# The third layer's setup of a four-layer cross-attention kernel, regrouped by token tile and by head

## The chip, the cores and the metric

The kernel runs on one core of a Trainium2 chip. The metric is the device time of one execution in microseconds (us). The engines are TensorE (PE in the profile, with PEld for its weight loads), VectorE (DVE), ScalarE (ACT), GpSimd (POOL) and SyncE (SP, which here only starts DMAs). They run side by side and wait for one another on semaphores.

## The reference, cut to what matters

Four gated cross-attention layers, each followed by a feed-forward part, work on x of 8 x 56 tokens by 128 features, with a context of 8 x 1500 tokens. The change lies in the attention of the third layer, between the second layer's experts and the loop over the context:

```python
x = layer_norm(ctx, ...)                     # per context token, done earlier in the kernel
latents = layer_norm(x_tokens, ...)
q = latents @ Wq                             # 448 x 512: 8 heads of 64
k, v = split(concat([x, latents]) @ Wkv)     # per head 64 wide
q = q / |q| * q_scale                        # norm of each token and head
k = k / |k| * k_scale
sim = einsum(q, k) * 8                       # masked softmax over 1500 + 56 keys
out = softmax(sim) @ v
```

The kernel never forms the keys in this loop. For head h it uses q_h (W_k,h c) = (W_k,h^T q_h) c, so each head's normalised query (64 rows) is multiplied once by that head's key weights (64 x 128), and the loop then multiplies the 128-row result with the normalised context. The norms of the keys are applied to the scores.

## The kernel before

The 448 tokens stand in 4 token tiles of 112 (`TT` = 112, `NT` = 4, `N` = 448); `H8` = 8 heads, `HD8` = 64, `D` = 128. `ps` is the matmul memory, 8 banks of 512 words per partition, indexed as `ps[partition, bank, column]`.

The setup of the third layer is one chain. DVE normalises the latents; PE turns them, DVE copies them to `xT`. PE multiplies `xT` with `w_q2` (token tile t to bank t) and then with `w_k2` (tile t to bank 4 + t). ACT squares the query tiles one by one into `big2`; DVE waits for all four query products (`product_in.next(4)`), sums the squares by head (4 reductions), ACT takes the root, DVE the reciprocal, and one DVE multiplication over all four banks (112 x 2048) writes the normalised queries to `big`. PE turns them by 16 transposes, feature chunk c (two heads) to bank c. In each chunk partitions 0 to 63 hold the even head of the pair and 64 to 127 the odd one; ACT copies partitions 64 to 127 and DVE partitions 0 to 63, each in one instruction over four banks, into `qT2` of 8 heads, whose other halves GpSimd has zeroed by a memset (`l2_zero`). Because of the zeros, the product for a head takes all 128 rows of `w_kT2[:, h // 2, :]`. The 8 products go to the 8 banks, signalled after the fourth and the eighth. ACT casts each to float16 (`qtT[:, 0]`), DVE subtracts that from the float32 product to get the float16 remainder (`qtT[:, 1]`). Ahead of its subtractions DVE also does the norms of the latents' own keys: a reduction of 112 x 2048, a maximum, ACT's root, a reciprocal.

Then comes the loop over 8 batches of 13 key tiles (`sim2`, `scale2`, the exponential, `pv2`, and GpSimd's sum of the probabilities `psum2`). Its first scores need both halves of `qtT` and the loads of the first batch (`l2_ld`), which SP starts once the latents are stored.

`op.next()` on PE waits for the next count of the semaphore `operand`, which DVE raises; `product_in.next()` and `act_in.next()` on DVE do the same for `product` (raised by PE) and `from_act` (raised by ACT). `ch.step` counts a DVE instruction, `signal(s)` waits for the counted ones and raises `s`. `keep_clock(n, k)` issues n float16 matmuls of 128 x 512 into bank k whose result nobody reads. Each engine works through its instructions in the order of the program. A float32 matmul stands in the trace as two instructions.

Of the kernel before, what the change touches and what calls it, by code (L numbers as in the profile page):

```python
# [11 lines left out]
ALU = mybir.AluOpType  # L12
# [3 lines left out]
D = 128  # L16
B = 8
S = 56
N = B * S
NT = 4  # L20
TT = N // NT
# [100 lines left out]

PRODUCT = {"latent_q": 14, "latent_k": 18, "latent_qT": 19, "queries2": 20, "queries3T": 27}

# [6 lines left out]

OPERAND = {"latentsT": 13, "x3T": 24}

# [59 lines left out]
def build(nc, io, out):  # L193
    ctx = ExitStack()
    with ctx:
# [3 lines left out]
        def sem(name):  # L199
            return ctx.enter_context(nc.semaphore(name))  # L200
# [164 lines left out]
        ctxT = carve([D, H8, N])  # L365
        qT2 = ctxT
        sscl = [carve([KP, N]) for _ in range(2)]
# [95 lines left out]
        ld_rn = sem("latent_key_norms_loaded")  # L463
        l2_zero = sem("l2_queries_zeroed")
        l2_kn = sem("l2_latent_key_norms")
# [244 lines left out]
        def _(pe):  # L710
# [365 lines left out]
            for w in (w_q2, w_k2):  # L1076
                for t in range(NT):
                    mm = pe.matmul(ps[0:TT, t if w is w_q2 else 4 + t, :], xT[:, TT * t:TT * t + TT], w,
                                   start=True, stop=True)
                    if w is w_q2 or t == NT - 1:  # L1080
                        mm.then_inc(product, 1)
            op.next()
            for c in range(4):
                for t in range(NT):
                    mm = pe.transpose(ps[0:D, c, TT * t:TT * t + TT], big[:, t, D * c:D * c + D],
                                      ident[0:TT, 0:TT])
            mm.then_inc(product, 1)
            op.next()
            for h in range(H8):
                mm = pe.matmul(ps[0:D, (4 + h) % 8, 0:N], w_kT2[:, h // 2, :], qT2[:, h, :], start=True, stop=True)  # L1090
                if h % 4 == 3:
                    mm.then_inc(product, 1)
            op.next()
# [215 lines left out]
        def _(act):  # L1309
# [179 lines left out]

            act.wait_ge(product, PRODUCT["latent_qT"])  # L1490
            act.wait_ge(l2_zero, 1)
            act.copy(qT2[64:D, 1::2, :], ps[64:D, 0:4, 0:N]).then_inc(from_act, 1)
            act.wait_ge(to_act, 3)
            act.activation(qss[:, 1, :], qss[:, 1, :], ACT.Sqrt).then_inc(from_act, 1)
            for half in range(2):
                act.wait_ge(product, PRODUCT["queries2"] + half)
                for h in range(4 * half, 4 * half + 4):
                    act.copy(qtT[:, 0, h, :], ps[0:D, (4 + h) % 8, 0:N]).then_inc(qt_hi, 1)
            with act.Fori(0, B // 2) as i:
# [80 lines left out]
        def _(pool):  # L1580
# [99 lines left out]
            rsqrt()  # L1680
            pool.memset(qT2, 0.0).then_inc(l2_zero, 1)

# [70 lines left out]
        def _(dve):  # L1753
# [4 lines left out]
            def tt(out, a, b, op):  # L1758
                return dve.tensor_tensor(out, a, b, op)  # L1759

            def over(col, shape):

                return col.unsqueeze(2).broadcast_to(shape)
# [482 lines left out]
            signal(lat_ready)  # L2246
            product_in.next(4)
            for t in range(NT):
# [6 lines left out]
            ch.link(dve.reciprocal(qss[:, 2, :], qss[:, 2, :]))  # L2255
            bigf = big.rearrange("p t (h d) -> p (t h) d", h=H8)
            tt(bigf, ps[0:TT, 0:4, :].rearrange("p t (h d) -> p (t h) d", h=H8),
               over(qss[:, 2, :], [TT, NT * H8, HD8]), ALU.mult).then_inc(operand, 1)
            product_in.next(2)
            dve.wait_ge(l2_zero, 1)  # L2260
            ch.step(dve.tensor_copy(qT2[0:64, 0::2, :], ps[0:64, 0:4, 0:N]))
            act_in.next(5)
# [5 lines left out]
            for h in range(H8):  # L2268
                if h % 4 == 0:
                    product_in.next()  # L2270
                dve.wait_ge(qt_hi, h + 1)
                ch.step(tt(qtT[:, 1, h, :], ps[0:D, (4 + h) % 8, 0:N], qtT[:, 0, h, :], ALU.subtract))
            signal(operand)

# [232 lines left out]
```

## Time and profile before

| | |
|---|---|
| device time, median of 3 runs | 846.31 us (844.57 to 850.4) |
| profiled execution: device time | 849.31 us |
| profiled execution: span from first to last instruction | 847.5 us, 15714 instructions |
| PE, PEld busy | 754.1 us (89%), 496.9 us (59%) |
| DVE, ACT, POOL busy | 608.8 us (72%), 411.9 us (49%), 338.3 us (40%) |
| mean granted TensorE clock | 0.940 of full speed |
| the third layer's setup, from the latents' first product to the loop's first scores | 383.13 to 407.45 us of the span |

Busy shares are averages over stages with different limits, so the change is read from its own stage: which instruction released the next, and when. Times in the rows are us from the start of the span. The granted clock is 1.00 at 2.4 GHz and 0.50 at 1.2 GHz.

### The profile page before, as it was taken

What the parts mean: (1) busy time and instruction counts of PE and PEld (TensorE: products, weight loads), DVE (VectorE), ACT (ScalarE), POOL (GpSimd) and SP (SyncE); (2) the same over time, 40 slices, a digit from 0 to 9 for tenths busy, and PEclk for the clock granted to TensorE, in tenths of its full rate; (3) what the DMA queues carried; (4) which work ended last, traced back from release to release, by engine and by line L of the source; (5) the groups of instructions that cost most, each with busy time, mean ns of one, the idle gap of its engine ahead of it and who ended that gap; (6) DMA issues with size and microseconds to landing.
All of it is one profiled execution on the core that took longest, in us unless ns stands there. A gap on an engine that the chain in (4) does not pass through costs nothing.

```text
span 847.5 us, 15714 instructions
## 1 busy us (share of the span) xinstructions
PE 754.1 (89%) x5632; PEld 496.9 (59%) x5632; DVE 608.8 (72%) x1264; ACT 411.9 (49%) x675; POOL 338.3 (40%) x271
## 2 busy tenths in 40 slices
PE   4699999996778988997899999997799998998997
PEld 3577777785445475653455555563346665655575
DVE  4889999997887755565655556658789997525653
ACT  2476666673465524424445444421127775834331
POOL 0665555553523601540587787732241211100111
PEclk9899999997998968999999999998959999998999
DMA  7256766532425530206022233006746677000320
GB/s 202 94 193 216 244 211 202 162 122 84 55 85 183 159 108 0 84 29 173 1 77 76 78 110 106 8 14 100 111 84 132 123 147 157 3 2 26 98 89 23
DMA packets 50582, 88.35 MB, mean 104 GB/s; under 512 B 17374, under 2 KB 34974, under 8 KB 50166
## 3 DMA queue, kind: packets, MB, share of 16 engines
q1 hardware_dynamic: 50518, 87.49, 38.4%
q8 instruction: 41, 0.67, 0.4%
q14 instruction: 23, 0.19, 0.1%
HBM read 61.97 MB, written 25.51 MB: 103 GB/s over the span
## 4 chain that ended last, share of the span: by engine, by line
PE 46%; DVE 38%; ACT 5%; POOL 4%; issue 4%; DMA 2%; SPq 0%; DVEq 0%; POOLq 0%; ACTq 0%
DVE arena L2360 9%; PE ps L1111 8%; DVE arena L1759 8%; PE ps L1101 6%; DVE rn L1914 4%; PE ps L1279 3%; DVE arena L1963 3%; PE ps L1044 3%; PE ps L1289 3%; DVE arena L1942 2%; PE ps L1216 2%; PE ps L1205 2%; DVE arena L1922 2%; POOL arena L1696 2%; PE ps L1057 1%
## 5 line engine op out<-in xcount | busy, mean ns | idle before, releaser
L1759 DVE TENSOR_TENSOR arena<-ps,arena 128x448 f32<-128x448 f32 (+7 forms) x138 | 83.4, 628 | 58.4 <-ACT arena L1564 20.6
L2360 DVE TENSOR_REDUCE arena<-ps 112x1 f32<-112x500 f32 x192 | 114.4, 668 | 9.0 <-PE ps L1188 9.0
L1696 POOL TENSOR_TENSOR arena<-arena 125x448 f32<-125x448 f32 x96 | 109.5, 1141 | 24.2 <-ACT arena L1509 21.2
L1111 PE MATMUL ps<-arena 125*128 125x448 f32 (+1 forms) x208 | 97.1, 548 | 1.4 <-ACT arena L1509 1.0
L1540 ACT ACTIVATE arena<-ps 125x896 f32<-125x896 f32 x96 | 87.3, 917 | 22.4 <-PE ps L1205 22.4
L1509 ACT ACTIVATE arena<-arena,kbias 125x448 f32<-125x448 f32 x96 | 63.7, 668 | 65.3 <-DVE arena L1759 46.3
L1759 DVE TENSOR_TENSOR arena<-ps,rn 125x448 f32<-125x448 f32 x96 | 59.3, 618 | 47.7 <-PE ps L1101 43.3
L1101 PE MATMUL ps<-arena 128*125 128x448 f16 (+3 forms) x312 | 77.8, 359 | 3.0 <-DVEq L1770 3.0
L1101 PEld LDWEIGHTS ps<-arena 128*125 128x125 f16 (+1 forms) x312 | 40.9, 135 | 57.2 <-issue 42.3
L803 PE MATMUL ps<-w_k2h,arena 128*125 128x512 f16 x288 | 67.8, 388 | 6.9 <-ACT arena L1345 5.2
L1673 POOL TENSOR_TENSOR arena<-arena 112x512 f32<-112x512 f32 x24 | 30.4, 1267 | 90.4 <-DVE arena L1759 90.3
L1345 ACT ACTIVATE arena<-ps 125x512 f32<-125x512 f32 x96 | 55.9, 597 | 14.1 <-PE ps L803 11.1
L1914 DVE TENSOR_REDUCE rn<-arena 125x8 f32<-125x512 f32 x96 | 58.2, 677 | 0.0
L803 PEld LDWEIGHTS ps<-w_k2h,arena 128*125 128x125 f16 x288 | 39.2, 139 | 30.4 <-ACT arena L1345 8.4
L1188 PE MATMUL ps<-arena 64*112 64x500 f16 x192 | 54.1, 437 | 3.1 <-DVE arena L2360 1.5
L1216 PE MATMUL ps<-arena 125*32 125x168 f32 x768 | 48.7, 323 | 5.4 <-issue 3.1
L1591 POOL TENSOR_TENSOR arena<-arena 112x4 f32<-112x4 f32 x9 | 9.3, 1029 | 109.4 <-DVE arena L1783 101.6
L826 PE MATMUL ps<-w_l,arena 128*125 128x256 f32 x192 | 43.9, 385 | 2.6 <-ACT arena L1372 2.6
L1111 PEld LDWEIGHTS ps<-arena 125*128 125x128 f32 (+1 forms) x208 | 37.8, 189 | 13.9 <-issue 8.4
L730 PE MATMUL ps<-w_k2h 128*128 128x512 f16 x192 | 45.5, 392 | 0.0
L1607 POOL TENSOR_TENSOR arena<-arena 128x500 f16<-128x500 f32 x24 | 29.3, 1222 | 40.7 <-ACT arena L1332 40.7
L1279 PE MATMUL ps<-arena 128*128 128x448 f16 x192 | 41.7, 370 | 3.7 <-DVE arena L1759 3.7
(307 smaller groups left out, 1469.8 us busy)
## 6 DMA issues: line engine op xcount, KB each, us to landing
arena<-in_ctxT SPq DMA_DIRECT2D x8, 750.0 KB, 7.9
d_cln<-arena SPq DMA_DIRECT2D x8, 750.0 KB
d_clnT<-arena SPq DMA_DIRECT2D x8, 750.0 KB
d_k<-arena SPq DMA_DIRECT2D x24, 250.0 KB
d_v<-arena SPq DMA_DIRECT2D x24, 250.0 KB
arena<-d_clnT SPq DMA_DIRECT2D x8, 750.0 KB
arena<-in_ctx SPq DMA_DIRECT2D x8, 672.0 KB
arena<-d_cln SPq DMA_DIRECT2D x8, 672.0 KB
```

The lines of the kernel that those rows point to most:

```text
L803: mm = pe.matmul(ps[0:KP, k, :], clnT[p][:, a, KP * j:KP * j + KP], w_k2h[:, w, :], start=(n == 0), stop=(n == 2))
L1101: mm = pe.matmul(ps[0:rows, (t + p) % 2, 0:N].rearrange("p (h q) -> p h q", h=H8), clnT_s[p][:, a, cols:cols + rows], qtT[:, q, :, bass.ds ...
L1111: pe.matmul(ps[0:D, 4 + 2 * p, 0:N], cln_s[p][0:rows, t, :], pexp[(t + p) % 2][0:rows], start=(t == 0), stop=(t == KT)).then_inc(l2_pv, 1)
L1216: pe.matmul(ps[32 * g:32 * g + 32, 6, 0:168], v3s[p][:, t, 32 * g:32 * g + 32], p3[t % 2][:, 3 * g:3 * g + 3, :].rearrange("p h q -> p (h ...
L1279: mm = pe.matmul(ps[0:D, 2 + 2 * (c % 2) + m, 0:N], wh3[p][:, w, at:at + D], xTh[:, a, :], start=(n == 0), stop=(n == 2))
L1345: act.activation(sqk[:, j % SQ, :], ps[0:KP, k, :], ACT.Square).then_inc(a_free, 1)
L1509: act.activation(pexp[(t + p) % 2][0:rows], sscl[(t + p) % 2][0:rows], ACT.Exp, bias=bias)\
L1540: act.activation(p3[t % 2].rearrange("p (k h) q -> p k (h q)", k=2), ps[0:KP, 2 * (t % 2):2 * (t % 2) + 2, 0:8 * S], ACT.Exp).then_inc(l3_ ...
L1696: ins = pool.tensor_tensor(psum2[p][0:rows], psum2[p][0:rows], pexp[(t + p) % 2][0:rows], ALU.add)
L1759: return dve.tensor_tensor(out, a, b, op)
L1914: dve.tensor_reduce(rn[:, bass.ds(turn - 1, 1), j, :].rearrange("p o h -> p (o h)"), sqk[:, j % SQ, :].rearrange("p (h d) -> p h d", h=H8) ...
L2360: dve.tensor_reduce(mx3[bn % 2][:, u % 2, u % 8 // 2, u // 8:u // 8 + 1], ps[0:TT, max_bank_of(bn, u), 0:500], AX.X, ALU.max).then_inc(l3_ ...
```

## The change

The setup is regrouped, with the same arithmetic except that products with zeros are gone:

- DVE no longer waits for all four query products ahead of the four reductions; each waits only for its tile's squares.
- The scaling of 112 x 2048 becomes four of 112 x 512, each signalled to PE.
- PE turns one token tile at a time (4 transposes into bank t), each tile signalled.
- The turned tiles are copied per tile into `qT2`, now 4 chunks with both heads of a pair packed into 128 rows: tiles 0 and 1 by ACT, tiles 2 and 3 by DVE, each 128 x 448. The memset and its semaphore are gone.
- The product of a head takes the 64 rows that hold it (`rows`), even heads partitions 0 to 63, odd heads 64 to 127, into bank h, and each head is signalled.
- ACT casts and DVE subtracts head by head as they are signalled; DVE signals PE after the fourth and after the eighth subtraction. Between these two signals stands `keep_clock(12, 2)` on PE.

```diff
@@ -120,7 +120,7 @@
 
 UNITS = [(b, 0) for b in range(B)] + [(b, third) for b in (7, 6, 0, 1, 2, 3, 4, 5) for third in (1, 2)]
 
-PRODUCT = {"latent_q": 14, "latent_k": 18, "latent_qT": 19, "queries2": 20, "queries3T": 27}
+PRODUCT = {"latent_q": 14, "latent_k": 18, "latent_qT": 19, "queries2": 23, "queries3T": 36}
 
 MAX_BANKS, TURN = (4, 5, 7), 24
 MAX_AHEAD = 32
@@ -129,7 +129,7 @@
     MAX_ORDER += [(_b, u) for u in range(4)] + [(_b - 1, TURN)] + [(_b, u) for u in range(4, 24)]
 MAX_ORDER.append((B - 1, TURN))
 
-OPERAND = {"latentsT": 13, "x3T": 24}
+OPERAND = {"latentsT": 13, "x3T": 28}
 
 
 
@@ -363,7 +363,7 @@
         qtT = carve([D, 2, H8, N], F16)
         latT = carve([D, 2, N], F16)
         ctxT = carve([D, H8, N])
-        qT2 = ctxT
+        qT2 = ctxT[:, 0:4, :]
         sscl = [carve([KP, N]) for _ in range(2)]
         pexp = [carve([KP, N]) for _ in range(2)]
         rnl = carve([S, B, H8])
@@ -461,7 +461,6 @@
         l2_s, l2_sc, l2_p, l2_pv = sem("l2_sim"), sem("l2_scaled"), sem("l2_probs"), sem("l2_pv_tile")
         l2_m = sem("l2_joined_matrices")
         ld_rn = sem("latent_key_norms_loaded")
-        l2_zero = sem("l2_queries_zeroed")
         l2_kn = sem("l2_latent_key_norms")
         l2_acc, l2_den = sem("l2_probs_added"), sem("l2_denominators")
         l2_done = sem("l2_batch_done")
@@ -1079,17 +1078,19 @@
                                    start=True, stop=True)
                     if w is w_q2 or t == NT - 1:
                         mm.then_inc(product, 1)
-            op.next()
-            for c in range(4):
-                for t in range(NT):
-                    mm = pe.transpose(ps[0:D, c, TT * t:TT * t + TT], big[:, t, D * c:D * c + D],
+            for t in range(NT):
+                op.next()
+                for c in range(4):
+                    mm = pe.transpose(ps[0:D, t, TT * c:TT * c + TT], big[:, t, D * c:D * c + D],
                                       ident[0:TT, 0:TT])
-            mm.then_inc(product, 1)
+                mm.then_inc(product, 1)
             op.next()
             for h in range(H8):
-                mm = pe.matmul(ps[0:D, (4 + h) % 8, 0:N], w_kT2[:, h // 2, :], qT2[:, h, :], start=True, stop=True)
-                if h % 4 == 3:
-                    mm.then_inc(product, 1)
+                rows = slice(64 * (h % 2), 64 * (h % 2) + 64)
+                pe.matmul(ps[0:D, h, 0:N], w_kT2[rows, h // 2, :], qT2[rows, h // 2, :], start=True, stop=True)\
+                    .then_inc(product, 1)
+            op.next()
+            keep_clock(12, 2)
             op.next()
 
             def sim2(b, p, t):
@@ -1487,15 +1488,15 @@
             for t in range(NT):
                 act.activation(big3[:, t, :], ps[0:TT, 4 + t, :], ACT.Square).then_inc(from_act, 1)
 
-            act.wait_ge(product, PRODUCT["latent_qT"])
-            act.wait_ge(l2_zero, 1)
-            act.copy(qT2[64:D, 1::2, :], ps[64:D, 0:4, 0:N]).then_inc(from_act, 1)
+            for t in range(2):
+                act.wait_ge(product, PRODUCT["latent_qT"] + t)
+                ins = act.copy(qT2[:, :, TT * t:TT * t + TT], ps[0:D, t, 0:N].rearrange("p (c n) -> p c n", c=4))
+            ins.then_inc(from_act, 1)
             act.wait_ge(to_act, 3)
             act.activation(qss[:, 1, :], qss[:, 1, :], ACT.Sqrt).then_inc(from_act, 1)
-            for half in range(2):
-                act.wait_ge(product, PRODUCT["queries2"] + half)
-                for h in range(4 * half, 4 * half + 4):
-                    act.copy(qtT[:, 0, h, :], ps[0:D, (4 + h) % 8, 0:N]).then_inc(qt_hi, 1)
+            for h in range(H8):
+                act.wait_ge(product, PRODUCT["queries2"] + h)
+                act.copy(qtT[:, 0, h, :], ps[0:D, h, 0:N]).then_inc(qt_hi, 1)
             with act.Fori(0, B // 2) as i:
                 for p in range(2):
                     b = 2 * i + p
@@ -1678,7 +1679,6 @@
                 pool.wait_ge(ex_acc, e + 2)
                 add_expert(e, e % 2)
             rsqrt()
-            pool.memset(qT2, 0.0).then_inc(l2_zero, 1)
 
             with pool.Fori(0, B // 2) as i:
                 for p in range(2):
@@ -2244,7 +2244,6 @@
             ch.link(dve.tensor_copy(latT[:, 0, :], xT))
             ch.step(tt(latT[:, 1, :], xT, latT[:, 0, :], ALU.subtract))
             signal(lat_ready)
-            product_in.next(4)
             for t in range(NT):
                 act_in.next()
                 ch.step(dve.tensor_reduce(qss[:, 0, H8 * t:H8 * t + H8],
@@ -2253,12 +2252,14 @@
             dve.tensor_scalar(qss[:, 0, :], qss[:, 0, :], 1e-24, None, ALU.max).then_inc(to_act, 1)
             act_in.next()
             ch.link(dve.reciprocal(qss[:, 2, :], qss[:, 2, :]))
-            bigf = big.rearrange("p t (h d) -> p (t h) d", h=H8)
-            tt(bigf, ps[0:TT, 0:4, :].rearrange("p t (h d) -> p (t h) d", h=H8),
-               over(qss[:, 2, :], [TT, NT * H8, HD8]), ALU.mult).then_inc(operand, 1)
-            product_in.next(2)
-            dve.wait_ge(l2_zero, 1)
-            ch.step(dve.tensor_copy(qT2[0:64, 0::2, :], ps[0:64, 0:4, 0:N]))
+            product_in.next(4)
+            for t in range(NT):
+                tt(big[:, t, :].rearrange("p (h d) -> p h d", h=H8), ps[0:TT, t, :].rearrange("p (h d) -> p h d", h=H8),
+                   over(qss[:, 2, H8 * t:H8 * t + H8], [TT, H8, HD8]), ALU.mult).then_inc(operand, 1)
+            product_in.next(3)
+            for t in range(2, NT):
+                product_in.next()
+                ch.step(dve.tensor_copy(qT2[:, :, TT * t:TT * t + TT], ps[0:D, t, 0:N].rearrange("p (c n) -> p c n", c=4)))
             act_in.next(5)
             signal(operand)
             ch.link(dve.tensor_reduce(qss[:, 1, :], big3.rearrange("p t (h d) -> p (t h) d", h=H8), AX.X, ALU.add))
@@ -2266,11 +2267,11 @@
             act_in.next()
             dve.reciprocal(qss[:, 1, :], qss[:, 1, :]).then_inc(l2_kn, 1)
             for h in range(H8):
-                if h % 4 == 0:
-                    product_in.next()
+                product_in.next()
                 dve.wait_ge(qt_hi, h + 1)
-                ch.step(tt(qtT[:, 1, h, :], ps[0:D, (4 + h) % 8, 0:N], qtT[:, 0, h, :], ALU.subtract))
-            signal(operand)
+                ch.step(tt(qtT[:, 1, h, :], ps[0:D, h, 0:N], qtT[:, 0, h, :], ALU.subtract))
+                if h % 4 == 3:
+                    signal(operand)
 
             def scale2(b, p, t):
```

## Rows read from the trace of the kernel before

**Rows 1.** Chain of waits, setup of the third layer: start us, duration us, what (xcount).

```profile
383.13 5.40 PE ps L1078 x8
...
388.55 2.48 DVE arena L2250 x4
...
391.27 0.24 ACT arena L1485
...
391.53 0.36 DVE arena L2255
...
391.92 2.30 DVE arena L1759
...
394.26 1.77 PE ps L1085 x16
...
396.05 2.03 DVE arena L2261
...
398.17 6.29 PE ps L1090 x16
...
405.12 2.23 DVE arena L1759 x4
...
407.45 2.52 PE ps L1101 x6
```

**Rows 2.** Timeline, ACT in the setup: start, us, engine, line, operation, operands [idle before].

```profile
389.17 1.28 ACT L1485 ACT_TABLE_LOAD   x1
...
391.99 2.06 ACT L1488 ACTIVATE arena<-ps 112x512 f32<-112x512 f32 x4 [0.49 <-PE ps L1078]
...
396.05 1.65 ACT L1492 COPY arena<-ps 64x1792 f32<-64x1792 f32 x1 [2.01 <-PE ps L1085]
...
401.48 1.84 ACT L1498 CAST arena<-ps 128x448 f16<-128x448 f32 x4 [0.51 <-PE ps L1090]
...
409.74 1.28 ACT L1509 ACT_TABLE_LOAD   x1 [3.42 <-DVE arena L1759]
```

**Rows 3.** Timeline, DVE and POOL in and just before the setup.

```profile
375.96 0.69 DVE L1759 TENSOR_TENSOR arena<-ps,arena 112x512 f32<-112x512 f32 x1
...
380.32 3.08 POOL L1681 MEMSET arena<- 128x3584 f32 x1
...
398.21 2.29 DVE L2264 TENSOR_REDUCE arena<-arena 112x32 f32<-112x2048 f32 x1
...
402.11 2.21 DVE L1759 TENSOR_TENSOR arena<-ps,arena 128x448 f16<-128x448 f32 x4 [0.76 <-ACT arena L1498]
```

**Rows 4.** Timeline, PE: 64-row products of an earlier stage beside 128-row ones.

```profile
319.94 2.05 PE L722 MATMUL ps<-arena 128*112 128x128 f32 x8 [0.34 <-ACT arena L1436]
321.92 2.08 PE L1025 MATMUL ps<-arena 64*128 64x128 f32 x16
```

**Rows 5.** Windows: stretch, length, busy of PE, PEld, DVE, ACT, POOL, then PEclk, DMA share, GB/s.

```profile
319.90:323.90 4.00, 3.96 (x24) 3.52 (x24) 1.80 (x4) 0.00 (x0) 0.00 (x0) 0.50 0.00 0
380.00:383.30 3.30, 1.42 (x8) 0.81 (x9) 2.22 (x8) 0.00 (x0) 3.30 (x2) 0.99 0.19 47
383.30:386.70 3.40, 3.40 (x5) 1.22 (x6) 0.97 (x2) 0.60 (x1) 0.10 (x1) 0.50 0.26 89
...
398.10:404.50 6.40, 6.28 (x16) 2.96 (x16) 5.03 (x7) 2.08 (x6) 0.00 (x0) 1.00 0.21 38
404.50:407.40 2.90, 0.00 (x0) 0.00 (x0) 2.22 (x4) 1.83 (x4) 0.00 (x0) 0.96 0.00 0
407.40:410.70 3.30, 3.25 (x9) 1.85 (x9) 1.25 (x2) 0.96 (x1) 0.00 (x0) 0.52 0.00 0
```

**Rows 6.** Timeline, PE's clock-keeping matmuls, and a loop step at full clock on PE and POOL.

```profile
374.21 5.78 PE L730 MATMUL ps<-w_k2h 128*128 128x512 f16 x26
...
419.77 5.23 POOL L1696 TENSOR_TENSOR arena<-arena 125x448 f32<-125x448 f32 x4
...
421.94 0.73 PE L1101 MATMUL ps<-arena 128*125 128x448 f16 x3
```

## The prediction, made before the changed kernel was run

> **What bounds the kernel now.** I read the chain of waits first, restricted to the setup and to the loop's start, because whole-kernel busy shares say nothing about a stage of 24 us. It alternates strictly between engines [rows 1]: PE forms the query products until 388.53, DVE reduces the squares until 391.03, ACT and DVE finish the norm by 391.89, DVE scales for 2.30, PE turns for 1.77, DVE copies for 2.03, PE multiplies for 6.29, then a cast and four subtractions until 407.35, and at 407.45 the loop's scores begin. So each engine waits for the whole of the step before it. The timeline then shows what runs beside the chain: ACT's squares, table load and copies [rows 2], DVE's own rows and GpSimd's memset [rows 3]. The windows show the granted clock [rows 5]: 1.00 during the products (2.4 GHz), and 0.52 in the 3.3 us in which the loop's first scores run (nearly all at 1.2 GHz), right after 2.9 us in which PE did nothing.
>
> In the loop, GpSimd's four sums in 5.23 and PE's step both have a period of about 1.32 us [rows 6], and nothing in the change touches them. The loop has 104 steps of that; whatever the start gains should be kept to the end.
>
> **The change part by part.**
>
> Reductions without the wait for all products. ACT's table load begins as its fourth square ends, at 389.17 [rows 2]. Four reductions take 2.48 back to back [rows 1], 0.62 each; the first three now finish between the squares, and the last runs 389.2 to 389.8. From the last reduction to the end of the reciprocal it is 0.86 (391.03 to 391.89), of which the root takes 0.24 and the reciprocal 0.36 [rows 1], so the maximum with all hand-overs 0.26; it ends at about 390.05. But ACT's table load occupies it until 389.17 + 1.28 = 390.45 [rows 2]; then root and reciprocal with two hand-overs give 391.1 against 391.89. Gain 0.8, not 1.2: the table load is late next.
>
> Scaling and turning by tile. One instruction took 2.30 [rows 1]. A single one of 112 x 512 takes 0.69 [rows 3], and four reductions of that size took 2.48 [rows 1]; four scalings therefore take between 2.30 (no cost for cutting) and 4 x 0.69 = 2.76. I take 2.5, the reductions being four of the same size on the same engine, back to back. The last tile is scaled at 393.6. Sixteen transposes took 1.77 [rows 1], so 0.11 each; the first three tiles' lie beside the scaling, and the fourth tile's 4 with their latency end about 0.65 later, 394.25. Here 1.4 us of turning goes off the path.
>
> The rows show a single 512-wide operation at 0.69 and a 2048-wide one at 2.29 [rows 3]. The Trainium skill ("VectorE: DVE Perf Modes", the section on the TRN2 errata) says that a fixed latency is paid by every VectorE instruction, once by one large tile and again by each of many small ones, and gives (N + 151) cycles at 0.96 GHz for a float32 add: estimated from it, 0.69 for 512 and 2.76 for four. That is the upper end of my bracket; by it the forecast would be 0.3 us later.
>
> Copies by tile. DVE's two tiles become ready at about 393.65 and 394.25; each copy of 448 columns costs at most the 0.55 of a 448-wide subtraction (four took 2.21 [rows 3]) and at least a quarter of 2.03 [rows 1]. DVE ends at about 394.85. ACT has the four squares of the keys ahead of its copies in its queue; they end at 391.99 + 2.06 = 394.05 [rows 2]. Two copies follow, between 0.41 (a quarter of 1.65) and 0.46 each (casts of the same size, four in 1.84) [rows 2]: with hand-overs ACT ends at 395.05 and is the later of the two. With the signal PE starts its products at 395.1 against 398.17. All gains so far are 3.05.
>
> The memset. Its 3.08 run from 380.32 to 383.40 beside the latents' layer norm and first product [rows 1, 3], and `qT2` is first touched at 396.05. Taking it away is worth nothing.
>
> Products of 64 rows. Before, 16 passes took 6.29, 0.39 each. The trace has the nearest relative: 16 float32 passes of 64 rows, alternating between the two halves, in 2.08, directly behind 8 passes of 128 rows and the same width in 2.05, both at granted clock 0.50 [rows 4, 5]. Per pass that is 0.13 against 0.26, so the halves overlap. At best the eight products take 3.2 to 3.4 us (395.1 to 398.4), at worst, without overlap, the same 6.3 (401.4). I take the first.
>
> Casts head by head, and who is late next. Now DVE is. Behind its signal at 395.05 still stand the latents' key norms: a reduction of 2.29 [rows 3], then maximum, root and reciprocal, 0.86 as above, 3.15 in all, so until 398.2. ACT's first cast stands behind that root and runs 397.9 to 398.45; casts take 0.46, DVE's subtractions 0.55 [rows 2, 3]. Eight subtractions from 398.5 take 4.4, until 402.9. The two half rounds before had gaps for casts and products; now the eight run through. In the case without overlap the last product ends at 401.4 and the cast and subtraction behind it at 402.6, so even then DVE stays the bound. Without the twelve added matmuls the scores would start at 403.0.
>
> The added matmuls. PE waits for the fourth subtraction (398.5 + 2.2 = 400.7, signalled 400.8) and then issues twelve. In the rows 26 of them take 5.78, 0.22 each at full clock [rows 6], so twelve take 2.7 and end at 403.5; at half clock, twice the spacing, 5.3, and they end at 406.1. Queued behind them is the first score product; everything in the loop waits for that. At full clock they cost 0.5 us over 403.0 and are the last thing on the path. Scores begin at 403.5 against 407.45: 3.95 earlier, of which 3.05 were there when the products began.
>
> What they buy. The first six score passes took 2.52 at half clock [rows 1], 1.26 for one product; three passes at full clock take 0.73 with their latency [rows 6]. Only the first product lies on the path, since behind its scaling ACT loads a table for 1.28 (409.74 [rows 2]) before the first exponential, which covers the second. Gain 0.6, at least 0 if the clock is low again and at most 0.7.
>
> Sum: 0.8 + 2.25 + 0.9 + 0.6 = 4.55 us. The table load ends at 411.02 before and at about 406.5 after. The profiled execution of 849.31 (847.5 of span and 1.8 around it) would become 844.8. It lies 3.0 above the median, and nothing in the setup explains that, so I apply the same difference to the median: 846.31 - 4.6 = 841.7.
>
> The loads of the first batch could end the gain. DMA engines are busy for 0.21 of the stretch from 398.1 to 404.5 and not at all from there on [rows 5]; if that 1.3 us stands at its start, both batches' loads are in by about 399.5, and the scores at 403.5 still find them. Cover left: about 3.5 us.
>
> **The rivals.**
>
> A, the clock falls in the gap that row overlap opens. PE would be idle from 398.4 to 400.8. For it speaks that the clock stood at 0.50 after a stretch of 3.3 us in which PE worked 1.42, and fell again after 2.9 us of nothing [rows 5]. Against it: the 2.1 us between turning and multiplying, behind 1.8 us of turning alone [rows 1], led to no fall. Then the twelve matmuls take up to 5.3 and end at 406.1, 1.35 earlier than 407.45; with some clock back by the first scores 1.4 to 2. Time: 844.6.
>
> B, slower. The halves do not overlap and the clock is low already when the products start, after a stretch of short turning bursts and a wait. The place is the product loop: 16 passes x 2 x 0.39 = 12.5 from 395.1, 407.6; then twelve matmuls at half clock, 5.3, 412.9, 5.4 after 407.45, and the scores at half clock as before: 851.7. It decides from 7 us of products on (407.45 - 5.3 - 395.1). The rows of the 64-row passes speak against it.
>
> C, the regrouping does not do what it says: the products do not overlap, the clock stays. Products end at 401.4, after the fourth subtraction's signal; the twelve end at 404.1. Gain 3.4 + 0.6 = 4.0: 842.3. This differs from the forecast by less than can be measured; the profile alone tells.
>
> D, the setup gains its 4 to 5 us but later stages meet the clock differently. Mean granted clock is 0.940, so about 100 us run at half rate, in many short stretches, and three runs of one kernel already spread over 5.8 us. A stretch like that of 383.3 to 386.7 [rows 5] costs up to 1.7, and one or two more or fewer of them move the total by 2 to 4 either way: 838 to 846.
>
> **How the numbers follow.** Forecast with clock and overlap as taken: 0.52. A 0.22, C 0.08, D 0.12, B 0.04, anything else 0.02. The likeliest case gives 841.7. The range goes down to 837.5 (forecast and a favourable D) and up to 846.3 (A with D against it); B stays out. A measurement of this kernel can tell about 1%, 8.5 us, from no change. Neither the forecast, A nor C reaches that; only D stacked on the forecast does on the fast side (0.07), and B with D on the slow side (0.04). Within 1%: 0.89.
>
> **What would show it.** In the changed profile: the four reductions interleaved with the squares, and the root directly behind the table load at about 390.5; four scalings about 0.6 apart with bursts of 8 or fewer transposes beside them; products starting 3 us earlier and 16 passes in 3.2 to 3.5 us; the last subtraction's signal ahead of the end of the twelve matmuls; the granted clock 1.00 in the loop's first scores. The prediction is wrong if the products take 6 us, if the twelve matmuls take over 3 us (rival A), if the DMA releases the first scores, or if the loop's steps are no longer 1.32 apart.

## The result

| | before | changed |
|---|---|---|
| median of 20 runs each | 849.35 us (844.55 to 854.56) | 845.7 us (842.05 to 850.46) |
| profiled execution: device time, span | 849.31, 847.5 us | 845.34, 843.6 us |
| mean granted clock | 0.940 | 0.943 |

The ratio of changed to before is 0.9957, 95% interval 0.9938 to 0.9976: 0.43% faster, a small gain that 20 runs of each can just tell from none.

The chain of waits of the changed kernel, same stretch as [rows 1]:

```profile
383.20 8.82 PE ps L1077 x16
392.01 1.72 PE ps L1084 x12
...
393.83 1.17 DVE arena L2262 x2
...
395.11 3.33 PE ps L1090 x16
398.43 0.39 DVE arena L1759
...
400.04 0.62 DVE arena L1759
...
400.76 4.30 PE ps L729 x12
405.06 1.15 PE ps L1102 x6
...
407.84 0.68 ACT arena L1510
```

The reductions and the scaling no longer stand in the chain as steps of their own; the products start at 395.11 and take 3.33 where they took 6.29. Behind them stand DVE's first four subtractions, and then, 4.30 us long, the twelve matmuls of `keep_clock(12, 2)`. What runs beside that chain is in the timeline:

```profile
389.24 1.28 ACT L1486 ACT_TABLE_LOAD   x1
389.25 0.69 DVE L2249 TENSOR_REDUCE arena<-arena 112x8 f32<-112x512 f32 x1 [0.17 <-ACT arena L1484]
...
390.53 0.23 ACT L1486 ACTIVATE arena<-arena 112x32 f32<-112x32 f32 x1
...
391.18 2.48 DVE L1759 TENSOR_TENSOR arena<-ps,arena 112x512 f32<-112x512 f32 x4
...
391.92 2.39 PE L1084 MATMUL ps<-cst,arena 112*128 112x112 f32 x16
...
395.14 2.29 DVE L2265 TENSOR_REDUCE arena<-arena 112x32 f32<-112x2048 f32 x1 [0.16 <-DVE arena L2262]
...
397.82 3.55 ACT L1499 CAST arena<-ps 128x448 f16<-128x448 f32 x8
...
400.76 4.30 PE L729 MATMUL ps<-w_k2h 128*128 128x512 f16 x12 [2.38 <-DVEq L1770]
...
400.86 2.21 DVE L1759 TENSOR_TENSOR arena<-ps,arena 128x448 f16<-128x448 f32 x4 [0.21 <-DVE arena L1759]
...
406.54 1.28 ACT L1510 ACT_TABLE_LOAD   x1 [5.17 <-DVE arena L1759]
```

DVE's last subtraction ends at 403.07, two microseconds ahead of the end of the twelve matmuls. The windows (columns as in [rows 5]) say why these are so long:

```profile
395.10:398.40 3.30, 3.28 (x16) 1.46 (x16) 2.82 (x3) 0.72 (x3) 0.00 (x0) 1.00 1.08 266
398.40:400.70 2.30, 0.00 (x0) 0.00 (x0) 2.22 (x4) 2.30 (x6) 0.00 (x0) 0.95 0.67 161
400.70:401.70 1.00, 0.94 (x3) 0.39 (x4) 0.84 (x2) 0.67 (x2) 0.00 (x0) 0.50 0.21 34
...
404.00:404.50 0.50, 0.50 (x4) 0.23 (x3) 0.00 (x0) 0.00 (x0) 0.00 (x0) 1.00 0.02 1
```

PE had nothing to do from 398.4 to 400.7, and in this execution the granted clock fell to 0.50 just before the matmuls that were to hold it up. It was back at 1.00 before they ended, and the loop's first scores ran at full clock (six passes in 1.15 us against 2.52 in [rows 1]).

The loop's first exponential starts at 407.84 against 411.04, 3.2 us earlier. The loop's 104 steps carry this over unchanged. GpSimd's last sum of the loop stands at

```profile
555.26 1.12 POOL L1696 TENSOR_TENSOR arena<-arena 56x448 f32<-56x448 f32 x1 [0.41 <-ACT arena L1510]
```

and ends at 556.38, that is 148.54 after the first exponential; before it was 148.54 as well (411.04 to 559.58).

### The profile page after: what moved, and what is told of

It is laid out like the page before. It is cut to its first block, busy times and chain, and to the rows that moved or that the text cites. A ratio compares the mean times of both kernels' runs of the same rounds, so it can differ in the third digit from the quotient of the medians.

```text
span 843.6 us, 15748 instructions
## 1 busy us (share of the span) xinstructions
PE 751.6 (89%) x5644; PEld 495.1 (59%) x5644; DVE 608.4 (72%) x1268; ACT 410.5 (49%) x676; POOL 335.4 (40%) x270
## 4 chain that ended last, share of the span: by engine, by line
PE 46%; DVE 37%; ACT 5%; issue 5%; POOL 4%; DMA 2%; SPq 0%; DVEq 0%; POOLq 0%; ACTq 0%
DVE arena L2361 9%; PE ps L1112 8%; DVE arena L1759 8%; PE ps L1102 6%; DVE rn L1914 4%; PE ps L1280 3%; DVE arena L1963 3%; PE ps L1043 3%; PE ps L1290 3%; DVE arena L1942 2%; PE ps L1217 2%; PE ps L729 2%; PE ps L1206 2%; DVE arena L1922 2%; POOL arena L1696 2%
## 5 line engine op out<-in xcount | busy, mean ns | idle before, releaser
L729 PE MATMUL ps<-w_k2h 128*128 128x512 f16 x204 | 49.9, 401 | 2.4 <-DVEq L1770 2.4
L1206 PE MATMUL ps<-arena 64*125 64x112 f16 x768 | 43.3, 233 | 4.1 <-issue 4.1
```

The lines of the kernel that those rows point to most:

```text
L729: pe.matmul(ps[0:D, k, :], w_k2h[:, 0, 0:D], w_k2h[:, 0, :], start=True, stop=True)
L1206: mm = pe.matmul(ps[0:KP, 2 * (t % 2) + r, 112 * g:112 * g + 112], kst[b % 3][rows, g, KP * t:KP * t + KP], qst3[rows, b:b + 1, g, 2 * r:2 ...
```

## The experiments

The setup's start moves from execution to execution (its first product begins at 383.13 before, 383.20 changed, 384.54 and 379.97 in two of the runs below). So the traces are compared from one event inside it, the start of the root's table load on ACT (389.17 before, 389.24 changed), called T0. All columns are read from each run's timeline; the ratio is that of the timed runs to the kernel before.

| kernel | T0 to products | products take | T0 to end of last subtraction | added matmuls | T0 to end of the loop's table load | ratio (95%) |
|---|---|---|---|---|---|---|
| before | 9.00 | 6.29 | 18.17 | none | 21.85 | 1 |
| before, again | 9.00 | 6.28 | 18.18 | none | 21.86 | one run, 844.89 us |
| changed | 5.87 | 3.28 | 13.83 | 12 in 4.30 | 18.58 | 0.9957 (0.9938 to 0.9976) |
| changed, again | 5.87 | 3.28 | 13.85 | 12 in 4.45 | 18.74 | 0.9973 (0.9946 to 1.0001) |
| no added matmuls | 5.87 | 3.28 | 13.84 | none | 17.12 | 0.9955 (0.9925 to 0.9984) |
| sixteen, early | 5.87 | 3.28 | 13.84 | 16 in 3.63 | 16.93 | 0.9963 (0.9935 to 0.9990) |
| even heads first | 5.87 | 6.58 | 14.14 | 12 in 2.76 | 17.91 | 0.9967 (0.9940 to 0.9994) |
| thirty | 5.87 | 3.28 | 13.85 | 30 in 8.34 | 22.62 | 0.9999 (0.9971 to 1.0027) |
| one scaling | 7.09 | 3.28 | 15.07 | 12 in 2.76 | 18.27 | 0.9961 (0.9934 to 0.9987) |
| memset back | 5.88 | 3.28 | 13.86 | 12 in 2.76 | 17.06 | 0.9963 (0.9941 to 0.9985) |
| signals by four | 5.87 | 3.28 | 13.85 | 12 in 4.26 | 18.55 | 0.9974 (0.9945 to 1.0004) |
| reductions wait | 6.65 | 3.28 | 14.63 | 12 in 2.76 | 17.83 | 0.9972 (0.9942 to 1.0002) |
| norms on GpSimd | 5.88 | 3.28 | 12.21 | 12 in 2.76 | 15.30 | 0.9906 (0.9877 to 0.9935) |
| norms split | 5.87 | 3.28 | 12.21 | 12 in 2.76 | 15.29 | 0.9924 (0.9892 to 0.9955) |

The ratios rest on 20 runs of the changed kernel, 6 of "norms on GpSimd" and 11 or 12 of each of the others. Their intervals reach 0.2 to 0.3% to either side, 1.6 to 2.7 us. Four of them hold 1 (again, thirty, signals by four, reductions wait). Against the changed kernel they part only "norms on GpSimd"; the interval of thirty matmuls still overlaps slightly. Single steps are told by the traces, where steps that don't depend on the clock agree to 0.02 us from run to run. In every one of these 14 profiles the loop took 148.54 or 148.55 from its first exponential to the end of its last sum.

What varies lies around the setup and the loop: T0 falls between 384.14 and 391.61 us in these profiles, and from the end of the loop's last sum to the end of the span it is 284.6 to 289.6. So a single span decides nothing: the second profile of the kernel before has a span of 843.1 us, less than the 843.6 of the changed kernel, with the waits of the setup as long as in the first.

**Without the added matmuls.**

```diff
             op.next()
-            keep_clock(12, 2)
             op.next()
```

> The changed kernel without the twelve added matmuls. In the changed kernel's profile they run 400.76 to 405.05, 4.30 us, because the clock had fallen by 400.7, and the last subtraction had been done by 403.1. Theory (DVE ends the setup, the twelve matmuls at half clock cost 2 us and buy the full clock back): scores begin at 403.1 at granted clock 0.50, the first product takes 1.4, the first exponential's table load ends at about 406.7 against 407.82; some of that 1.1 us goes back in the loop's first steps at half clock, so the total is 0 to 1 us below the changed kernel (ratio to before 0.9945 to 0.9957). Rival (the matmuls earn their place): the loop's first 3 or 4 us at half clock cost more than they do, total 1 to 2 us above the changed kernel, ratio 0.997 to 0.998.

Against the changed kernel the loop's table load ends 1.46 earlier from T0, more than the 1.1 expected, and nothing is given back in the loop. The time alone doesn't decide (0.9955 is what the theory had, but the interval holds the rival's 0.997 to 0.998 too); by this trace the rival fell. PE was idle for 4.7 us, and the first nine passes of scores ran mostly at half clock:

```profile
399.70:404.40 4.70, 0.00 (x0) 0.00 (x0) 4.43 (x8) 2.97 (x7) 0.00 (x0) 1.00 0.30 46
404.40:408.00 3.60, 3.17 (x9) 1.60 (x9) 1.25 (x2) 1.61 (x2) 0.00 (x0) 0.58 0.00 0
404.40:405.00 0.60, 0.46 (x3) 0.39 (x4) 0.00 (x0) 0.00 (x0) 0.00 (x0) 0.99 0.00 0
```

Only one product of scores stands ahead of ACT's table load, and the third window shows that the clock fell when half of that product was through, 0.45 us after its start. Where it falls differs from execution to execution, so this was in part luck. From the last subtraction to the end of the loop's table load it is 3.28 here, 3.20 with twelve matmuls at full clock (memset back), 4.75 with twelve at half clock (changed), and 3.68 in both profiles of the kernel before, where the clock had fallen ahead of the scores. So against this profile the twelve are worth 0.08 at full clock and cost 1.47 when the clock falls under them; against a low clock from the first score on, as in the kernel before, they are worth 0.48 and cost 1.07. One profile of the version without them can't say which is usual.

**Sixteen matmuls, early.**

```diff
-            keep_clock(12, 2)
+            keep_clock(16, 0)
...
-                if h % 4 == 3:
+                if h in (0, 7):
                     signal(operand)
```

> The changed kernel with DVE's first signal after the first subtraction instead of the fourth, and sixteen matmuls into bank 0 behind it instead of twelve into bank 2. Theory (the fall comes from the 2.3 us in which PE has nothing to do between the products and the fourth subtraction): PE idles only 398.4 to 399.1, the granted clock stays 1.00, sixteen matmuls take 3.6, end before the last subtraction's signal at 403.1; scores begin at 403.1 at full clock, the first table load ends at 406.0, 1.8 us ahead of the changed kernel; ratio to before 0.9936. Rival (the fall has another cause, such as the 64-row products themselves): clock 0.50 from about 400 all the same, sixteen matmuls take up to 7, scores at about 405 to 406, no better than the changed kernel.

```profile
393.52 0.62 DVE L1759 TENSOR_TENSOR arena<-ps,arena 128x448 f16<-128x448 f32 x1
394.26 3.63 PE L729 MATMUL ps<-w_k2h 128*128 128x512 f16 x16 [0.79 <-DVEq L1770]
...
398.28 1.35 PE L1102 MATMUL ps<-arena 128*125 128x448 f16 x6 [0.39 <-DVEq L1770]
```

PE idles 0.79 instead of 2.38, sixteen matmuls take 3.63, DVE's signal releases the scores, all as the theory had it; the table load ends 1.65 ahead of the changed kernel from T0, but only 0.13 ahead of the profile in which the twelve met the full clock and nothing else was slower (memset back, 17.06). That the early place keeps the clock up is not shown by this one profile, since behind the gap of 2.38 it stayed up three times in seven as well; with the two versions of the norms below it is three profiles of three. The timed ratio of 0.9936 that was expected lies just inside the interval, the measured 0.9963 doesn't show the gain: 1.65 us is less than such a measurement resolves.

**Even heads first.**

```diff
-            for h in range(H8):
+            for h in (0, 2, 4, 6, 1, 3, 5, 7):
                 rows = slice(64 * (h % 2), 64 * (h % 2) + 64)
```

and the same order for casts and subtractions.

> The changed kernel with the heads of products, casts and subtractions in the order 0,2,4,6,1,3,5,7, so that neighbouring products use the same 64 rows. Theory (neighbours on different halves of the rows overlap, and that overlap is what opens the idle gap): products take 6.2 to 6.4 instead of 3.33, end at 401.4, PE does not idle, the clock stays 1.00, the twelve matmuls take 2.7, scores begin at 404.1 against 404.9; total 0.8 us below the changed kernel or the same. Rival (the overlap is what the change gains by): the scores come 2 to 3 us later and the total is 2 to 3 us above the changed kernel, ratio 0.998 to 0.999.

The products take 6.58, but that isn't the price without overlap alone. PE's weight loads show passes on the same half 0.38 us apart while the clock was 1.00; from 395.68 on loads come in pairs, by their number the first odd heads beside the last even ones, and much of that part ran at half clock:

```profile
394.93 0.19 PEld L1090 LDWEIGHTS ps<-arena 64*128 64x128 f32 x1 [0.19 <-issue]
395.30 0.19 PEld L1090 LDWEIGHTS ps<-arena 64*128 64x128 f32 x1 [0.19 <-issue]
...
396.18 0.55 PEld L1090 LDWEIGHTS ps<-arena 64*128 64x128 f32 x2 [0.19 <-issue]
396.93 0.55 PEld L1090 LDWEIGHTS ps<-arena 64*128 64x128 f32 x2 [0.20 <-issue]
```

What the low clock cost and what the pairs gave back nearly cancel. That neighbours on different halves overlap in the changed kernel is shown by its own trace, where the weights of two passes at a time are loaded 0.38 apart:

```profile
395.59 0.19 PEld L1090 LDWEIGHTS ps<-arena 64*128 64x128 f32 x2 [0.18 <-issue]
395.96 0.19 PEld L1090 LDWEIGHTS ps<-arena 64*128 64x128 f32 x2 [0.18 <-issue]
```

The sixteen passes take 3.28 us there; those of the kernel before, 0.38 apart one by one, took 6.28, both at granted clock 1.00. With the even heads first PE goes straight on, the matmuls take 2.76, and the table load ends 0.67 before that of the changed kernel (0.8 expected), although the products are half as fast. The clock is not as the theory had it: it fell inside the products, 1.8 us after their start,

```profile
395.50:396.00 0.50, 0.50 (x3) 0.31 (x3) 0.50 (x1) 0.00 (x0) 0.00 (x0) 0.92 1.08 237
396.00:396.50 0.50, 0.50 (x4) 0.32 (x2) 0.47 (x2) 0.00 (x0) 0.00 (x0) 0.50 1.03 258
```

and came back within them. PE had idled only 0.79 ahead of them. So the gap behind short products is a place for the fall, not its only cause. Halving the products' time was worth 0.3 on DVE's last subtraction (13.83 against 14.14), because DVE was busy elsewhere for most of it.

**Thirty matmuls.** `keep_clock(30, 2)` for `keep_clock(12, 2)`.

> The changed kernel with thirty matmuls for twelve: a known delay of 18 x 0.22 = 3.9 us at full clock in the last step of the setup. Theory (what the setup gains or loses is carried to the end one for one): scores begin at about 408.9, the span grows by 3.9 us, the total is back at that of before, ratio 0.999 to 1.001. Rival (the loop or a later stage takes up a shift of the setup, and the measured gain is from elsewhere): the total grows by under 1.5 us, ratio under 0.9975.

The thirty took 8.34, 4.04 more than the twelve, the table load ended 4.04 later, and the ratio went from 0.9957 to 0.9999, back to the time before. That is 3.6 us by the medians, give or take 2.9: it agrees with a shift of the setup being paid one for one at the end, and the loop's 148.54 says so for the loop. The span of this profile, 843.1, is no longer than the changed kernel's 843.6, because its T0 happened to lie at 384.14, 5.1 us earlier.

**One scaling.**

```diff
-            for t in range(NT):
-                tt(big[:, t, :]..., ps[0:TT, t, :]..., over(qss[:, 2, H8 * t:H8 * t + H8], ...), ALU.mult).then_inc(operand, 1)
+            tt(big..., ps[0:TT, 0:4, :]..., over(qss[:, 2, :], ...), ALU.mult).then_inc(operand, NT)
```

> The changed kernel with DVE's four scalings of 112 x 512 put back into one of 112 x 2048 that signals all four tiles at its end; the turning stays by tile. Theory (what cutting gains is the turning of three tiles beside the scaling): from the root's table load to the start of the products it is 7.0 us instead of 5.87 (one scaling 2.29 for 2.48, then all sixteen transposes 1.8 of which only the copies of the first tiles overlap); the total 0.5 to 1.2 us above the changed kernel. Rival (cutting costs in fixed latency what it gains): 5.9 or less.

7.09 against 5.87: cutting the scaling is worth 1.22 to the start of the products, after paying the 0.19 that four instructions take more than one (2.48 for 2.29).

**The memset back**, over the whole of `ctxT`, with both waits for it.

> The changed kernel with GpSimd's memset of 128 x 3584 and the waits for it back ahead of the copies. Theory (it was hidden): table load to products 5.87 as without, the 3.1 us of memset end 10 us before the copies; total as the changed kernel, ratio to before 0.995 to 0.997. Rival (the memset slowed DVE's work on the latents beside it): the cast of 128 x 448 beside it takes 0.53 instead of 0.39 and the setup starts 0.1 to 0.3 us later.

5.88 to the products: hidden, as said. The rival's detail is half right: the cast of the latents, which begins beside the memset, is slower with it, 0.53 in the three profiles that have the memset against 0.39 or 0.40 in the others, and off the path. DVE's four instructions of 112 x 128 ahead of it, beside the memset as well, take 1.14 with and without it, and from their start to the setup's first product it is 2.67 in both, so the setup does not start later.

```profile
383.18 0.39 DVE L2244 CAST arena<-arena 128x448 f16<-128x448 f32 x1
```

is the changed kernel's; with the memset it is

```profile
383.24 0.53 DVE L2247 CAST arena<-arena 128x448 f16<-128x448 f32 x1
```

**Products signalled by four.**

```diff
-                    .then_inc(product, 1)
+                if h % 4 == 3:
+                    mm.then_inc(product, 4)
```

> The changed kernel with the products signalled after the fourth and the eighth head, as before, instead of each. Theory (DVE's key norms hold casts and subtractions back until the products are almost done, so signals by head are worth nothing): first cast at 8.58 after the root's table load, eighth subtraction ends at 13.85, as in the changed kernel; total the same, ratio 0.994 to 0.998. Rival (handing over head by head is what shortens the second half of the setup): casts or subtractions wait for products and the last subtraction ends 0.5 to 1.5 later.

Last subtraction at 13.85, the same. Head by head buys nothing as long as the key norms stand first.

**Reductions wait for all products.** `product_in.next(4)` back ahead of them.

> The changed kernel with the wait for all four query products back ahead of DVE's four reductions. Theory (the wait is worth 0.8, as the table load is late next): products start 6.65 to 6.7 after the root's table load instead of 5.87; total 0.8 above the changed kernel, not to be told from it by time. Rival (the reductions were not on the path): 5.87 again.

6.65: the wait is worth 0.78.

**Key norms on GpSimd.** With DVE's signal after head 0 and twelve matmuls into bank 0:

```diff
             rsqrt()
+            pool.wait_ge(from_act, 15)
+            for w in (32, 16, 8, 4, 2):
+                ch.link(pool.tensor_tensor(sq[:, :, 0:w], sq[:, :, 0:w], sq[:, :, w:2 * w], ALU.add))
+            ch.link(pool.tensor_tensor(qss[:, 1, :], sq[:, :, 0], sq[:, :, 1], ALU.add))
+            ch.link(pool.tensor_scalar(qss[:, 1, :], qss[:, 1, :], 1e-24, None, ALU.max))
+            pool.tensor_tensor(qss[:, 1, :], qss[:, 1, :], nhalf[0:TT, :], ALU.pow).then_inc(l2_kn, 1)
...
-            ch.link(dve.tensor_reduce(qss[:, 1, :], big3..., AX.X, ALU.add))
```

> The changed kernel with the norms of the latents' own keys taken from DVE's and ACT's queues and done by GpSimd (six additions that halve the squares, maximum, power of -0.5, idle engine until then), DVE's first signal after the first subtraction, and the twelve matmuls into bank 0 behind it. Theory (the 3.15 us of key norms stand ahead of the casts and subtractions and set the end of the setup once the products are short): casts begin when the first product is out, 1.0 after the products' start, the eight subtractions end 6.0 after it instead of 7.9, scores begin 15.7 - 3.5 = 12.1 to 12.3 us after the root's table load (changed kernel 15.7, early matmuls 13.95) at granted clock 1.00; ratio to before 0.991 to 0.994. Rival (the products or casts bind next, or GpSimd's norms come late and hold the loop): scores later than 13.5 after the table load, or the loop's 13th tile waits for the norms.

```profile
395.81 5.42 POOL L1683 TENSOR_TENSOR arena<-arena 112x1024 f32<-112x1024 f32 x5 [13.76 <-ACT arena L1489]
396.73 3.28 PE L1090 MATMUL ps<-arena 64*128 64x448 f32 x16 [0.79 <-DVEq L1775]
397.78 3.59 ACT L1497 CAST arena<-ps 128x448 f16<-128x448 f32 x8 [1.19 <-PE ps L1090]
...
401.64 0.29 POOL L1685 TENSOR_SCALAR arena<-arena 112x32 f32<-112x32 f32 x1
402.01 5.46 POOL L1686 TENSOR_TENSOR arena<-arena 112x32 f32<-112x32 f32 x1
```

Now the casts begin 1.05 after the products' start (2.71 in the changed kernel), the last subtraction ends at 12.21, and the scores at 12.33 find the clock at 1.00. The setup is 6.55 us shorter than before by the loop's table load, and the ratio is 0.9906. Against "sixteen, early", which signals at the same place, 1.63 us of that are the norms' own (16.93 to 15.30). Here short products should pay. No run has the norms moved and the products slow, so this is not shown, but an estimate can be taken from "even heads first": there the last product ended at 12.45 after T0 and the last subtraction 1.69 behind it, at 14.14, so with such products the norms' move would have brought next to nothing, and with short ones it brings the last subtraction to 12.21.

**Norms split**: as that, with the root on ACT behind its casts and the reciprocal on DVE behind its last signal.

> The version with the key norms off DVE's queue again, without the one slow piece: GpSimd does the halving additions and the maximum, ACT the root behind its eight casts, DVE the reciprocal behind its last signal (in the version with all of it on GpSimd the power of 112 x 32 took 5.46 and held GpSimd's first sum of the loop until 16.59 after the table load, 0.5 late). Theory: scores at 12.3 to 12.4 and the loop's table load at an end of 15.3 after the root's table load as in that version, GpSimd's first sum at 16.0 to 16.1; ratio to before 0.989 to 0.993. Rival (the piece on GpSimd was hidden too, or the root behind the casts delays the loop's table load): 15.3 becomes 15.6 or more, ratio as the other version's or worse.

GpSimd's first sum comes at 16.15 instead of 16.59, but the loop's table load at 15.29 and the loop's 148.54 are the same: the late start of GpSimd was taken up within the loop. The split gains nothing. Both versions beat the kernel before. By the traces both also beat the changed one, by 3.3 us where its matmuls met half clock and by 1.8 where they met the full clock (memset back, 17.06); by the time only the first does, and the interval of the split overlaps with the changed kernel's.

**Both kernels again.**

> The changed kernel once more, for its time in the same job and for how the clock falls in another execution. Theory (where the clock falls within the setup differs from run to run, and the twelve matmuls take 2.7 or 4.3 to 5.3 with it): table load to products 5.87, to the last subtraction 13.8 again; the twelve matmuls anything between 2.7 and 5.3. Rival (the fall belongs to the gap of this kernel each time): 4.3 again, clock 0.50 from the fourth subtraction on.

> The kernel before once more, for a second profile. Theory (the clock falls at different points of the setup from run to run, the waits are the same): root's table load to products 9.0, to the last subtraction 18.2, the first scores at granted clock 0.50 or 1.00. Rival (the fall in the 2.9 us before the scores belongs to the kernel): 0.50 again.

The waits repeat to 0.02 us. Before again fell to half clock ahead of the first scores; the changed kernel again had its twelve matmuls at half clock, 4.45. Over the seven profiles in which PE waited the same 2.38 us ahead of these matmuls (changed, again, thirty, one scaling, memset back, signals by four, reductions wait) twelve took 2.76 three times and 4.26 to 4.45 three times, and of the thirty the windows show 0.51 from 396.60 to 400.00. In two of the four the clock fell in the gap, 0.27 us (changed) and 0.34 us (signals by four) ahead of the matmuls; in the other two it fell only 0.73 us (again) and 0.99 us (thirty) after they had begun. The rival that the fall belongs to this gap each time is wrong, and so was I to leave it at one chance in five.

## Why the prediction was wrong, and what of it held

Two steps failed. The first is the term of the twelve added matmuls: "At full clock they cost 0.5 us over 403.0 and are the last thing on the path", with the full clock taken as the likelier case, 0.52 against 0.22 for rival A. In the changed kernel's profile they met half clock, took 4.30 instead of 2.7 and ended at 405.05 instead of 403.5, beyond the 3 us that the prediction itself had named as its sign of being wrong. The second is what a measurement can tell: the forecast was to stay below it ("can tell about 1% ... Neither the forecast, A nor C reaches that"), and the measured 0.43% is a gain with an interval clear of none.

The forecast was a gain of 4.6 us; measured are 3.65, with an interval from 2 to 5.3. Of the 4.0 us between the forecast 841.7 and the measured 845.7, 3.0 are the base from which the gain was taken off and 0.95 the gain. The steps, from T0 or as durations:

- Reductions: 0.8 with the table load late next. 0.78, and the root began at 390.53, directly at the table load's end.
- Scaling in four: 2.5 was taken between 2.30 and 2.76. It is 2.48: one alone takes 0.69, but they lie 0.60 apart. The Trainium skill ("VectorE: DVE Perf Modes", the errata section) has each of many small tiles pay the fixed latency, and the 2.76 estimated from it was not reached; by this trace part of it is paid beside the neighbour.
- Products to start at 395.1: 395.11, and at 5.87 or 5.88 from T0 in every run that leaves this part as it is. ACT was taken as the later of the two with its copies, at 395.05; the chain goes by DVE's, but both ended within 0.02 us of each other, at 394.97 and 394.99.
- Products of 64 rows in 3.2 to 3.4: 3.28.
- DVE as the next bound, with last subtraction at 402.9: 403.07. I named the cast-by-head signals with it without pricing them apart; they are worth nothing.
- Memset at nothing: nothing.
- The twelve matmuls, the step that failed: rival A, given 0.22, came in four of seven profiles, though milder than priced (4.3 to 4.45, not 5.3, since the clock came back before their end). With them at full clock the loop's table load ends 4.79 us ahead of before (21.85 - 17.06), where 4.55 were summed; at half clock 3.1 to 3.3.
- What they buy: 0.6 was booked for the clock and 0.5 as their cost. From the last subtraction to the end of the loop's table load it was 3.68 before, and is 3.09 where the clock is up and no matmul is in the way (sixteen, early): the 0.6 is right. With the twelve in between at full clock it is 3.20, so they cost 0.1 there, not 0.5. A run without them can come out nearly as well (3.28), when the clock falls late.
- The base: I took the median of three runs, 846.31, and moved the profiled time down by 3.0. Over 20 runs the median before is 849.35, what the profiled execution had shown; the 844.8 that the sum gave for that execution was the better forecast for the 845.7 measured.
- "A measurement of this kernel can tell about 1%": with 20 runs of each it told 0.43% from none. The move is inside 1%, as forecast with 0.89, and yet a measured gain; the text should have said that the forecast itself, 0.5%, would show with enough runs.

Rivals B and C fell with the 3.28 of the products. D, a clock that later stages meet differently, is not needed for the gain: of the 3.9 us by which the two profiled spans differ 3.2 stand at the loop's start and 0.7 behind the loop. But the stages outside do differ from execution to execution by as much as the change is worth, in one and the same kernel too: between the two profiles of the kernel before 3.3 us stand behind the loop (287.9 and 284.6) and 1.1 ahead of T0. How much of that is the clock I did not follow up. That the median's 3.65 lies so near the 3.1 to 3.3 of the traces at half clock is in part luck, with an interval from 2 to 5.3.

## What to carry to other kernels

Cutting a chain of whole-array steps into tiles pays where the next engine can start on the first tile (1.2 us here for the turning). A product made twice as fast pays little while the engine behind it is busy: look for work that nobody waits for at once, here 3.1 us of norms in DVE's queue, and move that to an idle engine first; that was worth 1.6 us, while signals by head were worth nothing. Matmuls that are to hold up the clock had better stand right behind the real ones: there the clock stayed up in three profiles of three, and behind a wait of 2.38 us in three of seven, and in the other four they ran at half rate on the path themselves. That is few profiles for a rule. And judge a change of a few microseconds by the steps of its own stage in two or more traces, since the spans of one kernel differed by 4.4 us here.

## What the runs showed of the hardware that was not expected

- The same program with the same waits meets the clock differently in each execution. With the same 2.38 us idle of PE ahead of the matmuls the granted clock fell to 0.50 in four profiles, within 0.34 us ahead of their start to 0.99 behind it, and not in three; 4.7 us of idle in one run left it at 1.00 until the next work had begun.
- The setup's first eight passes took 5.38 us (5.35 in one) or 3.69 by the clock alone (3.69 in three of the 14 profiles, those of "changed, again", "sixteen, early" and "thirty"), and their start differed by 5.8 us between profiles (379.80 in that with thirty matmuls, 385.57 in that with signals by four).
- One GpSimd power of 112 x 32 took 5.46 us, the maximum of the same size 0.29.
- In the run with even heads first, passes on the same 64 rows start 0.38 apart at granted clock 1.00, as those of 128 rows do in the kernel before: half the rows save nothing by themselves. In the same run two passes start together at 395.68, after four others. The four even heads stand first in the program with eight passes, so a pass of an odd head started before all of the even ones had. This is inferred from the starts, since the profile doesn't name a pass's head; 0.38 is the least seen here between passes on one half.
